# Gathers of two groups issued behind one wait on GpSimd, in a two-layer graph network on one Trainium2 core

## The reference, cut to what matters

```python
msgs = z[edge_dst] @ Wd + z[edge_src] @ Ws + edge_weight[:, None] * ww[None, :] + bm
agg = jax.ops.segment_max(msgs, edge_dst, num_segments=n)
agg = jnp.where(deg[:, None] > 0, agg, 0)
hidden = jax.nn.relu(z @ W1a + agg @ W1b + b1)
x = _layernorm(x + hidden @ W2 + b2)
```

## Time and profile before

| what | us |
|---|---|
| median of 3 executions | 1111.27 |
| lowest and highest | 1111.0, 1111.51 |
| span of the profiled execution | 1381.6 |
| busy in it: PE, PEld | 1108.2, 804.5 |
| busy in it: DVE, ACT, POOL | 819.0, 672.5, 740.7 |

### The profile page before, as it was taken

How to read it: one execution, slowest core, us unless ns; L and a number is a source line. 1 busy time by engine, 2 the same in 40 slices (tenths; PEclk the granted TensorE clock), 3 DMA queues, 4 the chain that set the end, 5 groups by cost and what they waited for, 6 DMA issues and landing times.

```text
span 1381.6 us, 24863 instructions
## 1 busy us (share of the span) xinstructions
PE 1108.2 (80%) x7041; PEld 804.5 (58%) x7041; DVE 819.0 (59%) x2919; ACT 672.5 (49%) x1736; POOL 740.7 (54%) x794
## 2 busy tenths in 40 slices
PE   4767788777787888688879788887687778889997
PEld 4445566565565665566556565555555546655777
DVE  5655656556565665656656555665566566565555
ACT  2323556666464765666556665642222222231465
POOL 4566666646555565555665556655666556600232
PEclk8876788888888999889989798998889889899999
DMA  6542323323322323323332223333334334234421
GB/s 165 137 116 75 74 67 87 73 76 80 81 68 70 94 75 86 76 72 87 86 100 64 70 73 95 92 83 72 74 79 111 87 74 121 77 114 142 131 60 45
DMA packets 126662, 121.23 MB, mean 88 GB/s; under 512 B 24238, under 2 KB 111077, under 8 KB 126517
## 3 DMA queue, kind: packets, MB, share of 16 engines
q1 hardware_dynamic: 99704, 69.74, 19.0%
q0 software_dynamic: 23712, 48.61, 14.7%
q10 hardware_dynamic: 3101, 1.21, 0.4%
HBM read 105.60 MB, written 13.88 MB: 86 GB/s over the span
## 4 chain that ended last, share of the span: by engine, by line
PE 44%; another core or an unknown queue 19%; DVE 18%; issue 12%; ACT 3%; SPq 1%; DMA 1%; ACTq 1%; DVEq 0%; POOL 0%; POOLq 0%
PE bank L1689 9%; DVE area L1255 5%; PE bank L1909 5%; PE bank L1679 5%; PE bank L1630 5%; DVE area L1239 5%; PE bank L1756 5%; PE bank L1784 4%; PE bank L1669 3%; DVE area L1238 3%; PE bank L1618 2%; DVE area L1240 2%; PE bank L1874 2%; PE bank L1712 1%
## 5 line engine op out<-in xcount | busy, mean ns | idle before, releaser
L1068 POOL DMA_INDIRECT area<-zs_d,area x721 | 690.4, 958 | 479.0 <-issue 177.6
L870 ACT CAST adj_w<-bank 128x325 f32 x391 | 176.5, 451 | 564.7 <-PE bank L1689 241.7
L1255 DVE TENSOR_TENSOR_SCAN area<-area,bank 128x512 f32<-128x512 bf16 x196 | 249.6, 1273 | 335.4 <-PE bank L1630 165.7
L1679 PE MATMUL bank<-area 128*128 128x325 bf16 x782 | 172.7, 337 | 166.3 <-DVE area L1240 121.0
L1238 DVE TENSOR_SCALAR area<-area 128x128 bf16<-128x128 f16 x782 | 205.2, 262 | 107.4 <-remote 95.9
L1689 PE MATMUL bank<-area 128*128 128x104 f32 x1564 | 261.0, 317 | 8.7 <-issue 5.5
L1239 DVE TENSOR_SCALAR area<-area 128x325 bf16<-128x325 f16 x782 | 243.6, 312 | 0.0
L1689 PEld LDWEIGHTS bank<-area 128*128 128x128 f32 x1564 | 229.5, 225 | 23.4 <-issue 6.8
L1679 PEld LDWEIGHTS bank<-area 128*128 128x128 bf16 x782 | 60.2, 103 | 203.9 <-DVE area L1240 134.3
L1784 PE MATMUL bank<-hot_r,zs_r 128*128 128x512 f32 (+1 forms) x450 | 152.0, 453 | 8.5 <-issue 7.1
L923 ACT ACTIVATE area<-adj_w,node_c 128x512 bf16<-128x512 f32 x225 | 154.9, 742 | 0.0
(11 more groups left out here) (174 smaller groups left out, 1086.3 us busy)
## 6 DMA issues: line engine op xcount, KB each, us to landing
area<-mask_d SPq DMA_DIRECT2D x195, 128.0 KB
area<-zs_d,area POOLq DMA_INDIRECT x721
area<-zs_d SPq DMA_DIRECT2D x640, 0.5 KB
area<-parts_d SPq DMA_DIRECT2D x20, 384.0 KB, 7.5
area<-wp_d SPq DMA_DIRECT2D x195, 9.0 KB
zr_d<-area SPq DMA_DIRECT2D x24, 128.0 KB
area<-zr_d SPq DMA_DIRECT2D x6, 512.0 KB, 4.2
area<-scale_d SPq DMA_DIRECT2D x10, 256.0 KB, 4.4
```

What stands on the lines that cost most here:

```text
L870: nc.scalar.copy(adj[:, :, bass.ds(at, W)], A_BANK[s % 2][:, 0:COLS].rearrange("p (h w) -> p h w", w=W))
L1068: pool.indirect_dma_start(gring[:, g % GR * 4 + s % 2 * 2 + u, :], None, x if g < RAW else zs_d[0:N, :], bass.IndirectOffsetOnAxis(ap=firs ...
L1255: nc.vector.tensor_tensor_scan(S[:, g % 2, 0:n], mask[:, g % MR, 0:n], (G_BANK if g in PICKED else T_BANK[g % 2])[:, 0:n], S[:, (g + 1) % ...
L1679: last = nc.tensor.matmul(o[:, 0:COLS], hot_l[:, r, u, :], hot_d[:, r, u, :], start=u == 0, stop=u == 1 and s == 0)
```

## The change

Group 9 waits as before. From group 10 on only even groups wait, for `t_ps` >= g-2, that is for the sums of group g-3, which free the slots of g and of g+1. Odd groups wait for nothing.

```diff
                 if GR <= g < GR + RAW:
                     pool.wait_ge(raw_ps, g - GR + 1)
-                elif g >= GR:
+                elif g == GR + RAW:
                     pool.wait_ge(t_ps, g - GR + 1)
+                elif g >= GR and g % 2 == 0:
+                    pool.wait_ge(t_ps, g - GR + 2)
```

## The result

| | median us | lowest to highest | executions |
|---|---|---|---|
| before | 1110.68 | 1106.58 to 1112.70 | 9 |
| after | 1116.47 | 1113.83 to 1119.18 | 9 |

The ratio is 1.0062, 95% interval 1.0049 to 1.0075: the change costs 0.6%, about 6.9 us (0.0062 x 1111). The forecast was +1.4 us.

What follows compares the result with a forecast made beforehand. Back-to-back gathers on GpSimd were taken to bound the kernel at 1111.3 us. Waits removed 0, room 0, behind picked groups 0, start 1.4 and burst 0 gave 1112.7 us, range 1110.4 to 1117.5.

Steps and rivals of the forecast that it cites:

- rival B: First gather after each picked group: TensorE over 3.1 us late there, 3.7 us, with the start 1116.4 us; chance 0.26.
- B's second reading: Same ending, slower by over 0.2%, from a loop start that costs 5 us rather than 1.4; chance 0.26 for both.
- Gathers set the pace: Unprofiled, GpSimd's gathers run back to back, one each 1.258 us, and every us it waits is a us of time.
- The sum 1111.3: Profiled span 1381.6 less 255.7 of GpSimd's waits and 14.6 after the last gather, against a median of 1111.27 us.
- Waits removed: 84 groups on GpSimd no longer wait; met waits cost nothing, so 0 us, -0.8 to +0.8.
- Burst of eight: Eight gathers in a row behind one wait bring nothing new to the DMA queues: 0 us.
- The start: Group 10 now needs group 7's sums and starts 1.4 us late, range 0 to 7.1; 0 of 5 us for group 12.
- Room of 8.1 us between picked groups: Even groups: how late TensorE may be before GpSimd waits, shrinking from 13.1 to 8.1 us; charged 0.
- TensorE at most 6.4 late: From groups 93 to 95 two groups took 16.46 us where gathers give 10.06; 6.4 us the upper end for one spell.
- Behind picked groups: Nine places where the room falls from 8.1 to 3.1 us; 0 to 7.7 us in all, 0 taken.
- still a slow execution: The profile after would be slow too, GpSimd's waits near 295 us in total and the span near 1381.
- C less the 0.8: Range's lower end, 1110.4: the rival that gathers don't bound the unprofiled execution (1111.3 us, chance 0.18), less the waits' grain.

Runs made afterwards that it cites:

- e6: Kernel before, with three gathers instead of four in groups 24, 28, ..., 192 (those not in `OWN`), 43 gathers fewer: ratio 0.9696, -33.7 us.
- e0: The kernel before, unchanged, run and profiled again: ratio 1.0001, +0.1 us, span 1109.5 us.
- e1: Kernel before, with even groups waiting for the sums of g-3 as in the change, odd groups keeping their own wait for g-4: ratio 1.0054, +6.0 us.
- e4: Changed kernel, with single waits as before in groups below 20 and in the four groups behind each picked group: ratio 1.0013, +1.4 us against before.
- e5: Changed kernel, with every group from 10 on, odd ones too, waiting for the sums of g-3: ratio 1.0037, +4.1 us against before.
- e7: Changed kernel, with SyncE's bulk load of slot 9 cut into seven pieces in slots 7 to 13: ratio 1.0035, +3.9 us against before.
- e3: Changed kernel, with single waits as before in the four groups behind each picked group: ratio 1.0041, +4.6 us against before.
- e9: Kernel before, with SyncE loading eight instead of four rows of a tile in each slot, 735 gathers instead of 741: ratio 1.2984, +331 us.

## Why the prediction was wrong, step by step

The time came out at 1116.47 where 1112.7 was forecast, and the change at +6.9 us where +1.4 was. The range held the time, but the chance of slower stood at 0.28 and that of the same at 0.66. The ending is that of rival B, which named 1116.4. That the number came so near is luck, since it charges 1.4 us to the start and 3.7 behind picked groups, and the runs have it the other way round; B's second reading, a start that costs 5 us, is nearer.

- *Gathers set the pace, and each us of GpSimd's wait is a us.* Right (e6, and the table, to some 2 us). The sum 1111.3 that stood for it fell within 2 us of e0's span, 1109.5, but by luck, since its parts cancel: the gather of group 9 starts at 62.41 us in e0, 6.5 earlier than the earlier trace rows, the stream lasts 1.6 longer than 886.9, from the last gather's end to the last scan it is 7.0 us and not 2.6, and 151.7 follow instead of 153.0.
- *Waits removed: 0.* Right, within what the runs can tell: e1 keeps them all and takes 0.9 us less than the change, interval of each about 1.5. Idle before a first gather is 0.30 in both. The Trainium skill's 50 to 100 ns for a semaphore read (Advanced Engine Details and Errata, Network/Comms) isn't seen; as an estimate from that page 84 waits less would have brought 4 to 8 us.
- *Burst of eight: 0.* Right (e1, e4).
- *The start: 1.4 of up to 7.1.* Right as far as it went. Group 10 is late by 1.35, 1.51, 1.72, 1.36, 1.68 and 1.38 us in six profiles, and no profile but the disturbed one has a wait at group 12, for which the prediction left out 5 us. The 15.06 us of the earlier trace rows between the transposes of groups 7 and 9, which it was taken from, belong to the disturbed execution: in them TensorE idled 6.37 us for VectorE's one-hots. In e0 the products ahead of these transposes are 7.1 us apart (67.66 and 74.80). But the start was followed to group 12 and no further.
- *Room of 8.1 us between picked groups, TensorE at most 6.4 late: 0.* This is the step that failed. Under it group 14 was charged nothing, and it has the largest wait, 2.2 to 2.9 us in four profiles (2.1 at group 13 in e5). In the prediction's terms TensorE is late at group 11 by 12.7 us in e0, the 15.9 above less the 3.2 that the prediction gave a group on time, and not by 6.4; and with a landing of 3.6 us the room is, as an estimate, 6.5 rather than 8.1. The 6.4 came from one spell at 600 us, and for groups 10 and 11 the prediction has no estimate of its own. The cause is the bulk load of slot 9, which e7 shows: TensorE idles for the weights of slot 10 for 5.6 to 7.4 us in all eleven profiles with that load in one piece, the first one of before apart. In the prediction's own profile it could be seen only in part. The load and the late product of slot 10 stand there, with about half the idle and no releaser named; TensorE was late there already:

```profile
81.49 0.72 PE L1679 MATMUL bank<-area 128*128 128x325 bf16 x2 [6.37 <-DVE area L1240]
...
84.65 3.56 SPq L580 DMA_DIRECT2D adj_w<-zs_d  x1
...
95.78 0.38 PE L1618 MATMUL bank<-area,ww 9*128 9x512 bf16 x1 [3.21 <-issue]
```

- *The same room from group 20 on.* Nearly 0: e4, in which 61 odd groups have no wait and their even neighbours the stronger one, costs +1.4 us (0.1 to 2.8), its excess being the two waits of 0.75 us at groups 20 and 108.
- *Behind picked groups: 0 of up to 7.7.* Too low. The table gives 2.3 us (after less e3), the profiles 2.6 and 0. The one large hit, 1.65 us, lay at the middle of 1.6; the other three were 0.2 to 0.4.
- *The profile after "still a slow execution", waits near 295 us, span near 1381.* Wrong. Both kernels profile at 1109 to 1115. A sign was there. SyncE's register moves of line 568, minimum, median and maximum in ns, in the profile of the prediction and in e0's:

```profile
L568 SPq MOVE area<-zs_d x640: 2/29/709, 69.5 to 1037.9; - x160
```

```profile
L568 SPq MOVE area<-zs_d x640: 29/29/39, 63.0 to 800.9; - x160
```

An instruction that takes 29 to 39 ns in e0, and 29 to 43 in e9, took 2 to 709 there. What disturbed that execution is open.

The range's lower end, "C less the 0.8", is 1110.5 and not 1110.4, which changes nothing.

The rule to issue a DMA early and to wait for it late (the Trainium skill, DMA: Bandwidth & Descriptors, Rules for kernel authors) had the sign: even groups are issued later, and the time went up by 0.6%.

## What to carry to other kernels

A ring that waits for one buffer more at a time costs little on the average slot (e4) and most at the few places where the consumer that frees the buffers is late: look for these first, one by one and the start above all, and follow each to its cause. A late transfer such as this one recurs in profile after profile. When a stream of equal instructions sets the pace, add up its idle beyond the fixed gap; that sum is the time to be had or lost, here to some 2 us. If the profiled execution is longer than the timed ones, compare an instruction of constant length before its waits are read.

## What the runs showed of the hardware

- A gather of 128 rows of 512 bytes holds GpSimd for 0.944 us (median) and the next starts 0.30 us later, with a met wait ahead of it or without: 1.25 us each, 721 of them 688 to 693 us of busy time in every profile. Where TensorE waited for its rows, they came 3.6 us after its start in the median (39 places of e0).
- After 6.2 to 7.0 us in which TensorE idled for a transfer (the changed kernel, e0), the clock granted to it was 0.50 (1.2 GHz) for the next 8.7 us, while it was busy for 8.67 and 8.66 of them. Four transposes took 1.11 us there instead of 0.66, so the wait cost more than its length. A long idle isn't needed for such a spell: at 500 us of the changed kernel 2.00 us of idle stand ahead of one.
- SyncE's loads of single rows by a register's value cost some 0.4 us each to issue; going from four to eight in a slot took SyncE's queue from 2% of the chain (e0) to 59% (e9) and made the kernel 30% longer.
- One load in seven pieces instead of two removed a wait of 2.5 us and, by the kernel before with it (+1.4 us, -0.1 to +2.9), may have cost some of it elsewhere.
